# Grouped attention: both output sums of a group in step seven, in place of one in step six and one in step seven

## What is computed

```python
groups = N_HEADS // N_KV_HEADS          # 16 // 4
q = (hidden_states @ Wq).reshape(B, S, N_HEADS, HEAD_DIM)
k = (encoder_hidden_states @ Wk).reshape(B, S_enc, N_KV_HEADS, HEAD_DIM)
v = (encoder_hidden_states @ Wv).reshape(B, S_enc, N_KV_HEADS, HEAD_DIM)
q = rms_norm(q, q_norm_w)
k = rms_norm(k, k_norm_w)
scores = jnp.einsum('bqhd,bkhd->bhqk', q, k) * scale
probs = jax.nn.softmax(scores, axis=-1)
out = jnp.einsum('bhqk,bkhd->bqhd', probs, v)
return out.reshape(B, S, N_HEADS * HEAD_DIM) @ Wo    # added to x
```

## Time and profile before

| | us |
|---|---|
| median of 3 executions | 1468.38 |
| fastest, slowest of them | 1464.65, 1472.4 |
| the profiled execution's own time | 1464.34 |
| its span in the trace | 1462.3 |
| mean granted clock of TensorE | 0.948 of full speed |

### The profile page before, as it was taken

One profiled execution on the slowest core, in us unless ns is written; L12 is line 12 of the kernel. 1 busy time (PEld: TensorE's weight loads), 2 busy tenths in 40 slices (PEclk: granted clock), 3 DMA queues, 4 the chain that ended last, 5 costly groups with the idle time before them and its releaser, 6 DMA issues. The chain is left out here.

```text
span 1462.3 us, 24088 instructions
## 1 busy us (share of the span) xinstructions
PE 1233.4 (84%) x8420; PEld 1098.3 (75%) x8423; DVE 1206.5 (83%) x2252; ACT 998.6 (68%) x1834; POOL 583.0 (40%) x419
## 2 busy tenths in 40 slices
PE   6898748888866798989999989999989999998645
PEld 5787727787755687878988978888878889887513
DVE  4666478889866889889899889899898998998477
ACT  3666327778854666778777777787777777787345
POOL 2433134434325443436425355344256253241144
PEclk9999859999997899999999999999999999999867
DMA  6232068899941877967777877877878777878510
GB/s 222 91 134 96 37 200 280 297 297 311 324 131 49 171 136 147 183 131 147 147 147 143 178 161 133 146 150 148 172 132 156 144 147 148 151 126 166 109 51 29
DMA packets 499696, 228.99 MB, mean 157 GB/s; under 512 B 441236, under 2 KB 479256, under 8 KB 499192
## 3 DMA queue, kind: packets, MB, share of 16 engines
q1 hardware_dynamic: 495016, 214.99, 64.4%
q0 software_dynamic: 4560, 12.46, 3.4%
HBM read 106.41 MB, written 11.93 MB: 81 GB/s over the span
## 5 line engine op out<-in xcount | busy, mean ns | idle before, releaser
L1934 ACT ACTIVATE ga_halves<-ga_probs,ga_inv_sum 128x1024 f16<-128x1024 f32 (+1 forms) x256 | 233.1, 957 | 160.3 <-DVE ga_inv_sum L2088 153.3
L2095 DVE SCALAR_TENSOR_TENSOR ga_halves<-ga_probs,ga_inv_sum,ga_halves 128x1024 f16<-128x1024 f32 (+1 forms) x256 | 321.5, 1256 | 0.5 <-issue 0.3
L1926 ACT ACTIVATE ga_probs<-ga_ps_s,ga_neg_max 128x1200 f32<-128x1200 f32 (+1 forms) x256 | 235.5, 928 | 64.9 <-DVE ga_neg_max L2080 64.5
L2075 DVE TENSOR_REDUCE ga_part_max<-ga_ps_s 128x1 f32<-128x1200 f32 x128 | 179.6, 1403 | 62.5 <-PE ga_ps_s L2122 62.3
L2122 PE MATMUL ga_ps_m<-ga_pT,ga_v 128*128 128x256 f16 (+1 forms) x1560 | 185.1, 274 | 0.0
L2122 PE MATMUL ga_ps_s<-side_kT,ga_qT 128*128 128x400 f32 (+1 forms) x768 | 158.8, 357 | 16.5 <-ACT ga_probs L1926 15.7
L2122 PE MATMUL ga_ps_s<-ga_kT,ga_qT 128*128 128x400 f32 (+1 forms) x768 | 159.7, 359 | 11.9 <-ACT ga_probs L1926 11.4
L2122 PEld LDWEIGHTS ga_ps_m<-ga_pT,ga_v 128*128 128x128 f16 (+1 forms) x1560 | 146.6, 98 | 30.6 <-issue 14.3
L2122 PEld LDWEIGHTS ga_ps_s<-side_kT,ga_qT 128*128 128x128 f32 x768 | 141.1, 195 | 21.6 <-ACT ga_probs L1926 18.7
L2122 PE MATMUL ga_ps_t<-side_w_kv,side_encT 128*128 128x256 f32 (+1 forms) x1170 | 154.6, 284 | 2.1 <-POOL ga_halves L1769 1.4
L2122 PEld LDWEIGHTS ga_ps_s<-ga_kT,ga_qT 128*128 128x128 f32 x768 | 141.5, 195 | 16.9 <-ACT ga_probs L1926 12.1
(11 more groups left out here) (294 smaller groups left out, 2517.0 us busy)
## 6 DMA issues: line engine op xcount, KB each, us to landing
ex_raw<-in_L_ffn_packed SPq DMA_DIRECT2D x63, 704.0 KB, 5.9
side_w_q_raw<-in_L_xattn_Wq SPq DMA_DIRECT2D x16, 512.0 KB, 3.7
side_w_q_raw<-in_L_xattn_Wo SPq DMA_DIRECT2D x16, 512.0 KB, 4.7
mix_y_rows<-ex_y SPq DMA_DIRECT2D x63, 128.0 KB, 4.4
side_enc<-in_ctx_turned SPq DMA_DIRECT2D x12, 512.0 KB, 5.0
ca_keys<-in_ctx_turned SPq DMA_DIRECT2D x12, 464.0 KB, 5.9
ca_cache<-in_ctx SPq DMA_DIRECT2D x4, 1024.0 KB, 7.1
ga_pT<-ga_halves SPq DMA_TRANSPOSE x256, 4.2
```

Of the source, the lines that this page charges most:

```text
L1926: nc.scalar.activation(dst, src, ACT.Exp, bias=neg_max[:, n % 2:n % 2 + 1], accum_out=half_sum[:, n % 4, k:k + 1]).then_inc(exped, 1)
L1934: nc.scalar.activation(halves[n % 2][:, HI, a:z], probs[n % PB][:, a:z], ACT.Copy, scale=inv_sum[:, n % 2:n % 2 + 1]).then_inc(high, 1)
L2075: nc.vector.tensor_reduce(part_max[:, 0:1], ps_s[:, 0:NB - 1, 0:WIDE], AX.XY, ALU.max)
L2095: nc.vector.scalar_tensor_tensor(halves[n % 2][:, LO, a:z], probs[n % PB][:, a:z], inv_sum[:, n % 2:n % 2 + 1], halves[n % 2][:, HI, a:z], ...
```

## The change

The list of jobs of a group's step 6 loses the sum of tile 0, and that of step 7 begins with both sums. The condition on the group stays, so this happens in groups 1 to 15, for the sums of groups 0 to 14. The sums of the last group, in the drain, are as they were.

```diff
@@ -1523,8 +1523,8 @@
                 7: []}[s]
         elif g < GROUPS and s == 0:
             jobs = [("qT", 1, g)]
-        if 0 < g < GROUPS and s in (6, 7):
-            jobs = [("y", s - 6, g - 1)] + jobs
+        if 0 < g < GROUPS and s == 7:
+            jobs = [("y", t, g - 1) for t in range(QT)] + jobs
         row, at = divmod(g + 2, G)
         if at == 0 and row < B:
             if s in (6, 7):
```

## The result

The changed kernel takes 1472.51 us (median of 20, 1467.19 to 1479.41) against 1468.26 us (median of 20, 1464.29 to 1472.4) for the kernel before. The ratio is 1.003, interval [1.0018, 1.0041]: 0.3% slower, or 4.25 us between the medians, with an interval of 2.6 to 6.0 us. The profiled execution has a span of 1465.3 us against 1462.3.

What follows compares the result with a forecast made beforehand. Step 7 was bound by the chain of maximum, bank emptying, sum 1 and next scores, step 6 not by TensorE. Terms +3.2, +1.3 and -0.6 gave +3.9 us on 1468.38, so 1472.3 us; range 1465 to 1480.

Steps and rivals of the forecast that it cites:

- Out of step 6, worth 0: Step 6: removing 12 products starts kT 2 and 3 1.5 us sooner, but scores still wait for the exponential; gain 0.
- The faster rival: Step 6 is TensorE's, so filling step 7's hole brings about 1.2 to 1.5 us a group: -16 us, 1452; chance 0.05.
- Into step 7, and the wait behind it, 0.32 us a plain group: Step 7: sum 0 fills the wait; sum 1 waits for kT 2's bank, released 0.32 us later, delaying the next scores.
- The additions, worth 0: Both VectorE additions fall in step 0's round; 0.42 us more there is hidden and q doesn't wait; cost 0.
- Groups 2, 6 and 10, -0.2 each: Where the clock fell, the second sum cuts idle time and it may hold; gain 0.2 us a group, between 0 and 1.35.
- Group 14, 1.3 us: Group 14, step 7: only 0.16 us of wait to fill, so two sums bring the scores later; cost 1.3 us.
- The sum, +3.9 us: Ten plain groups +3.2, group 14 +1.3, groups 2, 6 and 10 -0.6, group 15 0: +3.9 us in all.
- The rival of the clock in step 6's gap: The new 1.5 us gap in step 6 makes the clock fall, 1.3 us a fall, up to 1485; chance 0.11.
- the sign that was named as wrong: A granted clock of 0.5 inside plain groups was listed among the signs that would show the forecast wrong.
- The clock where a row begins: Rival: the clock holds in groups 2, 6 and 10, 1.35 us each in place of 0.2, so 1468.8; chance 0.10.

Runs made afterwards that it cites:

- first kernel with the shared bank: Kernel before, with both sums in halves of one bank, tile 0 in step 6, tile 1 in step 7, one addition: 1468.43 us against 1468.39.
- the second: Both sums in step 7 as in the changed kernel, but in halves of one bank with one addition: 1465.48 us against 1469.61 for the kernel before.

## Why the prediction was right

*Out of step 6, worth 0.* Right. The interval from step 6 to 7 is 7.29 before and 7.27 after. The faster rival needed step 6 to be TensorE's. It is not. One reading was wrong without a cost: the working has `kT` 2 and 3 start 1.5 us sooner. Counted from the last part of the maximum, `kT` 2 starts 1.4 us sooner, but `kT` 3 only 0.8 (0.87 us after it, 1.64 before), since the ring now makes it wait for the bank of `kT` 0. The working followed the ring for the sums and `q` and not for `kT` 3. The gap had room for this wait; in a step that TensorE sets it would have been a loss.

*Into step 7, and the wait behind it, 0.32 us a plain group.* Right: 0.31 in the interval from step 7 to 0, and 0.30 over the group. That this wait for `kT` 2's emptying is the loss is shown from two sides: kT 3's shorter emptying takes off 0.46 us, and a shared bank, which needs none, 0.5. The working gave TensorE as free at 749.07 and so only a short wait, 0.20 us, before the second sum. The weight loading waited 0.46 us, and without a wait the scores came 0.45 us sooner. So TensorE was free some 0.25 us sooner than the modelled ends say. That did not touch the forecast, since the release set the time.

*The additions, worth 0.* Right: `q` and `kv` don't wait for them in a plain group, and the interval from step 0 to 1 is 7.77 in both.

*Groups 2, 6 and 10, -0.2 each.* The mechanism was right, with the clock held and its gain stopped at GpSimd's weights. The size was 0.03 in place of 0.2, as the change in these groups alone showed (18.49 against 18.52 us). The working took TensorE's 0.24 us before `kv` as the gain. But those 0.24 us already were the wait for GpSimd's weights, which end at 873.27, 0.10 us before `kv` starts. There was nothing to be had while that part stays where it is.

*Group 14, 1.3 us.* The sign and the cause were right, the size 0.95 us. The term was put near its upper end. Counted from the last part of the maximum, the sums start 0.46 us sooner than the one sum did (0.10 for 0.56), where the working allowed 0.16, so the 0.25 us that a modelled end may hide were real. And the two sums take 2.96 us and not 3.08: 1.38 - 0.30 - 0.12 = 0.96.

*The sum, +3.9 us.* By the steps it is now 10 x 0.30 + 0.95 - 0.1 = +3.9 us as well: the two errors of size, 0.35 too much and 0.5 too little, and the 0.2 too much on plain groups nearly cancel. That they cancel is luck, and so is how near the total came: 1472.3 lies 0.2 us from a median whose distance from the kernel before is known to some 2 us. Measured are 4.25 us between the medians and 2.9 us between the first and last maximum of the two profiled executions (897.97 and 900.91 us), in which groups 0 and 1 and group 15, which differ between executions of the same code, were together 0.8 us shorter than the steps give.

*The rival of the clock in step 6's gap.* In groups 3 to 13, apart from those where a row begins, no trace of the 13 shows a granted clock of 0.5. Group 1, which the sum counted as plain, shows it around step 5 in all of them, the kernel before too, so there the sign that was named as wrong says nothing about the change.

*The clock where a row begins.* In groups 2, 6 and 10 with the sums apart the granted clock fell to 0.5 (1.2 GHz) in 8 of 12 places (the kernel before and three experiments), with both sums in step 7 in 5 of 27. The interval from step 7 to 0 is 8.68 to 8.71 us wherever it held and 9.30 to 10.51 wherever it fell. The Trainium skill, "TensorE: Matmul & The Clock Gate", Part 1, says that activity releases the throttle. The counts agree with that: with 1.5 us more of products between the two waits of TensorE a fall is rarer, though not ruled out.

## What to carry to other kernels

A wait that shows on an engine is worth its length only if that engine also sets the step in which the work is taken away. Read the maximum's rhythm, or another once-a-step instruction, on both sides of the move before counting it. In a ring of buffers, moving a job changes which buffer the jobs behind it need: ask who empties that one, how long that takes, and whether a shorter job can stand in its place. Here exchanging two jobs in the list was worth more than the move.

## What the runs showed that I had not expected

The stage before this one, whose code is the same in all kernels, ended between 463.0 and 473.2 us in thirteen profiled executions, counted to the first maximum. That spread is larger than the effect, and the intervals inside the stage, in most traces equal to a few hundredths of a microsecond from plain group to plain group, told what the totals could not.

GpSimd's part of the kv weights takes 2.24 to 2.35 us in some places and 1.26 to 1.29 us in all others, with the same operands. What tells the places apart is VectorE. In the second attention of the 13 traces the instruction starts 24 times while a low part on line 2095 is running on VectorE, and these are the slow ones, with two such parts beside it for 2.0 to 2.1 us. The other 158 times it starts before them or away from them, and 1.29 us is the longest, though some have up to 0.93 us of a low part beside them that began later. It is not the place behind the encoder part that makes it slow. It stands there in 27 of the 182 cases, and in three of these (groups 6 and 10 of the first kernel with the shared bank, group 10 of the second) the clock fell, VectorE came later, and it takes 1.28 to 1.29 us. Group 6 of the first (line 2103 is the low part here):

```profile
875.04 2.19 POOL L1790 TENSOR_TENSOR side_encT<-side_enc,side_encT 128x1024 fp32r<-128x1024 f32 x1 [5.16 <-ACT side_encT L1894]
...
877.19 1.28 POOL L1784 TENSOR_TENSOR side_w_kv<-side_w_kv_raw,side_w_kv 128x512 fp32r<-128x512 f32 x1
...
878.13 1.42 DVE L2103 SCALAR_TENSOR_TENSOR ga_halves<-ga_probs,ga_inv_sum,ga_halves 128x1024 f16<-128x1024 f32 x1
```

So about 1.0 of the 2.25 us of this instruction in the changed kernel, for which `kv` waits, comes with the low parts beside it, and putting the kv weights first also moved it ahead of them. The Trainium skill, "SBUF — State Buffer", on the two separate sides of SBUF, says that GpSimd and a VectorE instruction with two SBUF inputs exclude each other on a shared port, and that the one that starts first has it. The low parts have such inputs, and the 24 and 158 cases agree with this. No run changed the overlap alone.
